# DLRM tower on one core: three field pairs of the first tile are selected by comparison instead of gathered, and the gathers are spaced from round 20 on

## What is computed

```python
e = jnp.stack([tbl_0[ids[:, 0]], ..., tbl_31[ids[:, 31]]], axis=1)   # (2048, 32, 64)
p, q = e[:, ids_x, :], e[:, ids_y, :]                                # all 496 pairs i < j
pw = jnp.einsum('bpi,pij->bpj', p, w)                                # a 64x64 matrix per pair
z = jnp.einsum('bpj,bpj->bp', pw, q)                                 # 496 numbers per row
h = jnp.concatenate([z, dense_ctx], axis=1)                          # 512 numbers
h = jnp.maximum(h @ W_top1 + b_top1, 0.0)                            # 512
h = jnp.maximum(h @ W_top2 + b_top2, 0.0)                            # 256
y = h @ W_top3                                                       # 1
```

## Time and profile before

| | |
|---|---|
| median of 3 runs | 857.16 us |
| the profiled execution's own time | 858.86 us |
| its span, first to last instruction | 857.1 us |
| PE busy | 777.4 us (91%) |
| DVE busy | 614.4 us (72%) |
| POOL busy | 558.9 us (65%), 512 gathers with a mean of 999 ns |
| ACT busy | 276.0 us (32%) |
| granted TensorE clock, mean | 0.98 |

### The profile page before, as it was taken

The page is one execution under the profiler, slowest core; times in us unless marked ns, Lnnn a source line. Parts: engine busy times, 40 slices in busy tenths (PEclk is TensorE's granted clock), DMA queues, the critical chain, the costliest instruction groups (busy, mean ns, idle before and its releaser), DMA issues. The chain is left out here.

```text
span 857.1 us, 10074 instructions
## 1 busy us (share of the span) xinstructions
PE 777.4 (91%) x3904; PEld 284.5 (33%) x3904; DVE 614.4 (72%) x514; ACT 276.0 (32%) x461; POOL 558.9 (65%) x564
## 2 busy tenths in 40 slices
PE   0167999999999968999998999999998999999988
PEld 0022333333333323333333333333333333333333
DVE  0045778777887855988976788888877689889840
ACT  1253323213345211512454322503444422511102
POOL 6777777777777777778877788878877881101000
PEclk9988999999999988999999999999999999999999
DMA  4512222223322236757879577757879477827400
GB/s 131 203 33 71 76 76 65 66 73 76 76 77 74 57 96 141 164 136 161 199 166 219 123 168 167 158 144 158 192 160 231 105 167 151 172 49 141 93 13 0
DMA packets 33846, 103.44 MB, mean 121 GB/s; under 512 B 10564, under 2 KB 10948, under 8 KB 27528
## 3 DMA queue, kind: packets, MB, share of 16 engines
q0 software_dynamic: 23296, 67.14, 38.7%
q1 hardware_dynamic: 10504, 35.67, 13.5%
HBM read 52.43 MB, written 0.01 MB: 61 GB/s over the span
## 5 line engine op out<-in xcount | busy, mean ns | idle before, releaser
L582 DVE TENSOR_TENSOR prod<-main_ps,quad_t 128x1024 f32<-128x1024 f32 x448 | 517.4, 1216 | 193.4 <-PE main_ps L476 193.1
L348 POOL DMA_INDIRECT emb<-in_tbl,idx x512 | 511.6, 999 | 158.7 <-issue 152.8
L475 PE MATMUL main_ps<-e_t,w_sb 64*128 64x512 f32 x992 | 467.8, 610 | 0.0
L476 PE MATMUL main_ps<-e_t,w_sb 64*128 64x512 f32 x992 | 467.8, 610 | 0.0
L475 PEld LDWEIGHTS main_ps<-e_t,w_sb 64*128 64x128 f32 x992 | 176.8, 188 | 245.7 <-issue 175.1
L510 PE MATMUL z_ps<-prod,const_sb 128*32 128x512 f32 x1456 | 190.4, 605 | 22.2 <-DMA prod<-prod 19.0
L476 PEld LDWEIGHTS main_ps<-e_t,w_sb 64*128 64x128 f32 x992 | 176.8, 188 | 0.0
L613 ACT ACTIVATE e_t<-x_ps 128x512 f32<-128x512 f32 x64 | 38.3, 599 | 337.8 <-PE x_ps L446 332.3
L624 ACT ACTIVATE quad_t<-x_ps 32x512 f32<-32x512 f32 x224 | 131.4, 587 | 2.7
L359 POOL DMA_DIRECT2D prod<-prod x48 | 47.1, 981 | 92.1 <-DVE prod L582 92.0
L446 PE MATMUL x_ps<-const_sb,emb 128*128 128x128 f32 x256 | 44.7, 300 | 52.9 <-DMA emb<-in_tbl,idx 52.9
(11 more groups left out here) (18 smaller groups left out, 110.6 us busy)
## 6 DMA issues: line engine op xcount, KB each, us to landing
prod<-prod POOLq DMA_DIRECT2D x48, 1024.0 KB, 8.3
w_sb<-in_w SPq DMA_DIRECT2D x65, 512.0 KB, 4.1
emb<-in_tbl,idx POOLq DMA_INDIRECT x512
w_sb<-in_w SPq DMA_DIRECT2D x1, 1024.0 KB, 12.5
z_sb<-in_ctx SPq DMA_DIRECT2D x32, 4.0 KB
idx<-in_ids SPq DMA_DIRECT2D x1, 192.0 KB, 10.1
const_sb<-in_const SPq DMA_DIRECT2D x1, 125.0 KB, 2.2
idx<-in_ids SPq DMA_DIRECT2D x1, 64.0 KB, 1.9
```

The source lines that it names most:

```text
L348: pool.indirect_dma_start(out=emb[:, PLACE[n] + s // 2, s % 2, odd * EMBED:(odd + 1) * EMBED], out_offset=None, in_=tables[f], in_offset=b ...
L475: nc.tensor.matmul(main_ps[:, slot, c], w_sb[LOW, u, :], e_duo(t, low)[LOW, :], start=True, stop=True)
L476: last = nc.tensor.matmul(main_ps[:, slot + 1, c], w_sb[UP, u, :], e_duo(t, up)[UP, :], start=True, stop=True)
L582: ins = nc.vector.tensor_tensor(prod[:, a:a + 2, :], main_ps[:, slot:slot + 2, :], quad_t[:, quad_slot(t, q), h:h + 1, :].to_broadcast([P, ...
```

## The change

The file is also tidied (the code for half-width tiles goes, `step` becomes `unit`, the ids are laid out in another order); these parts issue the same instructions. What differs:

- Duos 13, 12 and 11 of the first tile are not gathered. SP loads their six tables whole (1000 or 1250 rows, 8 or 10 rows to each of 125 partitions) and their ids, one row spread to all partitions, into buffers that the MLP uses later. For each of the 8 or 10 rows that a partition holds, DVE compares 512 ids with that row's number (`compare_duo`, 125x512, 50 of them), which gives ones and zeros in the last quarter of `prod`. PE multiplies 125x64 of the table by it (`select_duo`) and sums over the rows in PSUM: in two banks of `main_ps` and in `z_ps`, which are not in use yet.
- The order in which the duos of the first tile are brought in becomes 13, 15, 12, 14, 11, 10, ... (`ARRIVE`); POOL gathers 15, 14, 10, 9, ...
- From round 20 of the first tile on POOL issues at most 4 gathers a round (before: from round 32 on).
- Rounds 0, 1, 4 and 6 of the second tile are folded by DMA too: 52 folds.
- The first MLP step waits for the last quarter of z and its context rows only ahead of its fourth matmul.

```diff
+COMPARED = (13, 12, 11)
+CHUNK = 125
+TABLE_ROWS = {26: 1000, 27: 1000, 24: 1250, 25: 1000, 22: 1000, 23: 1000}
+OH_PAIRS = 4
+OH_STEPS = [(m, k, [x for x in range(2) if k < CHUNKS[2 * m + x]]) for m in COMPARED
+            for k in range(max(CHUNKS[2 * m], CHUNKS[2 * m + 1]))]
+ARRIVE = (13, 15, 12, 14, 11, *range(10, -1, -1))
...
-UNFOLDED = {0: range(32), 1: (0, 1, 2, 3, 4, 6, 11, 19, 27), 2: (3, 11, 19, 27), 3: (3, 11, 19, 27, 30, 31)}
+UNFOLDED = {0: range(32), 1: (3, 11, 19, 27), 2: (3, 11, 19, 27), 3: (3, 11, 19, 27, 30, 31)}
...
-POOL_GATHERS = 4
+FREE_ROUNDS, POOL_GATHERS = 20, 4
...
-                    for _ in range(min(room, POOL_GATHERS) if a >= NGROUP else room):
+                    for _ in range(room if NGROUP * t + n < FREE_ROUNDS else min(room, POOL_GATHERS)):
...
+            def load_compared(i):
+                m = COMPARED[i]
+                at = TILE * COMPARED_FIELDS.index(2 * m)
+                sp.dma_start(z_flat[:, at:at + 2 * TILE].bitcast(I32), ids_c[i:i + 1, :].partition_broadcast(P)).then_inc(compare_in[i], 16)
+                for f in (2 * m, 2 * m + 1):
+                    sp.dma_start(table(f), tables[f].rearrange("(p k) e -> p (k e)", p=CHUNK)).then_inc(compare_in[i], 16)
+
+            sp.dma_start(idx[:, 0, :], ids[:, 0, :]).then_inc(idx_in[0], 16)
+            sp.dma_start(const_sb[:, :], const).then_inc(const_in, 16)
+            load_compared(0)
+            load_compared(1)
             load_weights(0)
-
-            sp.wait_ge(gathered[0], GATHERED[0])
+            load_compared(2)
+
+            sp.wait_ge(gathered[0], 16 * DUO_GATHERS)
...
+            def select_duo(m):
+
+                pe.wait_ge(compare_in[COMPARED.index(m)], 3 * 16)
+                bank = duo_bank(0, m)
+                mine = [i for i, step in enumerate(OH_STEPS) if step[0] == m]
+                for i in mine:
+                    _, k, xs = OH_STEPS[i]
+                    pe.wait_ge(hot_made, OH_MADE[i])
+                    for x in xs:
+                        f = 2 * m + x
+                        last = nc.tensor.matmul(bank[EMBED * x:EMBED * x + EMBED, :], table(f)[:, EMBED * k:EMBED * k + EMBED], hot(i, x),
+                                                start=(k == 0), stop=(k == CHUNKS[f] - 1))
+                    last.then_inc(hot_used, 1)
+                pe.wait_ge(hot_used, mine[-1] + 1)
+                pe.nop(nofuse=True).then_inc(transposed, 1)
...
-                        if n == 0 and k == 0:
-                            pe.wait_ge(z_out, Z0[t + 1])
...
+                        if n == 0 and k in (0, KTILES - 1):
+                            pe.wait_ge(z_out, KTILES * (t + 1) - (k == 0))
+
+                            rows = len([g for g in STARS if (g // ROUNDS_KT == KTILES - 1) == (k == KTILES - 1)])
+                            pe.wait_ge(ctx_in[k == KTILES - 1], 16 * 2 * rows * (t + 1))
...
+            def compare_duo(m):
+
+                if m == COMPARED[0]:
+                    dve.wait_ge(const_in, 16)
+                dve.wait_ge(compare_in[COMPARED.index(m)], 3 * 16)
+                for i, (d, k, xs) in enumerate(OH_STEPS):
+                    if d != m:
+                        continue
+                    if i >= OH_PAIRS:
+
+                        dve.wait_ge(hot_used, i - OH_PAIRS + 1)
+                    for x in xs:
+                        f = 2 * m + x
+                        at = P + 122 + IOTA[CHUNKS[f]] + k
+                        nc.vector.tensor_scalar(hot(i, x), compared_ids(f)[0:CHUNK, :], const_sb[0:CHUNK, at:at + 1], None, ALU.is_equal)\
+                          .then_inc(hot_made, 1)
```

More of the change, by code:

```diff
@@ L8 @@
 P = 128
[L9 to L12, removed]
+TILE = 512
+TILES = BATCH // TILE
+SUBS = TILE // P
 DUOS, QUADS = FIELDS // 2, FIELDS // 4
@@ L178, in order_events @@
     for t in range(TILES):
[L179 to L183, removed]
+        at, last = {}, 0
+        for m in ARRIVE if t == 0 else range(DUOS - 1, -1, -1):
+            j = DUOS - 1 - m
+            if t == 0:
+                n = max(min(FIRST_DUO[m] - 1, unit0(DUO_AT[j] + 1) if j > 12 else NUNIT), 0)
+            else:
+                n = min(unit0(NGROUP * t + DUO_AT[j]), NUNIT * t + FIRST_DUO[m])
+            at[m] = last = max(n, last)
             put(at[m], ("duo", t, m))
@@ L408, in _ @@
                 if kind == "end":
[L409 to L413 removed]
+                    part = PARTS_TILE * t + n // 2 + W_PARTS
+                    if n % 2 and part < PARTS_TILE * TILES:
+                        load_weights(part)
@@ L438, in transpose_duo @@
             def transpose_duo(t, m):
[L439 to L452 removed]
+                n = RING[t, m]
@@ L477, in main_products @@
[L477 to L490 removed]
+                elif n == MAIN - 1:
+                    pe.wait_ge(evicted, max(EVICTED["duo", 0, m] for m in COMPARED[:2]))
@@ new lines, in main_products @@
+                slot, w = 2 * (n % MAIN), (NGROUP * SLOTS4 * t + SLOTS4 * g + p) % W_SLOTS
+                kind, what = GROUPS[g]
+                if kind == "low":
+                    low = up = what[p % 2][0]
+                else:
+                    low, up = (side[0] // 2 for side in star_units(*what)[p])
+                nc.tensor.matmul(main_ps[:, slot, :], w_sb[LOW, w, :], e_duo(low)[LOW, :], start=True, stop=True)
+                nc.tensor.matmul(main_ps[:, slot + 1, :], w_sb[UP, w, :], e_duo(up)[UP, :], start=True, stop=True).then_inc(mains, 1)
@@ L547, in _ @@
             pe.wait_ge(const_in, 16)
-            for kind, a, b in EVENTS:
-                if kind == "duo":
-                    transpose_duo(a, b)
-                elif kind == "step":
-                    main_products(a, b)
+            for kind, t, n in EVENTS:
+                if kind == "duo" and (t, n) in RING:
+                    transpose_duo(t, n)
+                elif kind == "duo":
+                    select_duo(n)
+                elif kind == "unit":
+                    main_products(t, n)
@@ new lines, in product @@
+                slot, s = 2 * (n % MAIN), prod_tile(G, p, 0)
+                nc.vector.tensor_tensor(prod[:, s:s + 2, :], main_ps[:, slot:slot + 2, :], e_q, ALU.mult).then_inc(products, 1)
+                if (t, g) in V_FOLDS and p == 3:
+                    dve.wait_ge(products, n + 1)
+                    s = prod_tile(G, 0, 0)
+                    nc.vector.tensor_tensor(prod[:, s:s + 4, :], prod[:, s:s + 4, :], prod[:, s + 4:s + 8, :], ALU.add).then_inc(v_folded, 1)
+            for kind, t, n in EVENTS:
+                if kind == "duo" and (t, n) not in RING:
+                    compare_duo(n)
+                elif kind == "unit":
+                    product(t, n)
```

549 lines of the change are left out of this document (244 added, 305 removed).

## The result

| | before | after |
|---|---|---|
| median of the runs, us | 857.72 (855.94 to 859.48, 4 runs) | 829.61 (828.68 to 830.96, 4 runs) |
| span / own time of the profiled execution, us | 857.1 / 858.86 | 826.7 / 828.68 |
| PE busy | 91% | 95% |
| gathers, DMA folds | 512, 48 | 488, 52 |
| POOL issues its first DMA fold at, us | 316.89 | 241.94 |

After over before is 0.9674, with a 95% interval of 0.9649 to 0.9698: 28.1 us, 3.3% faster. Forecast: 833, range 823 to 849. The two profiled executions lie further apart, 30.2 us: that of after is the fastest of its four, and that of before is 1.7 us over the median that the prediction started from.

A forecast was written before the change was run, and what follows sets the result against it. POOL's queue up to the last fold PE waits for (654.79), then landing and PE alone, was taken as the bound: 857.1 - 35.0 + 4.6 + 9 - 2.4 = 833.3, forecast 833 us, range 823 to 849.

The forecast's parts named there:

- Gathers, 35.0 us: POOL's queue: 28 fewer gathers ahead of the folds, at 1.25 us each, bring the folds 35.0 us earlier.
- Four folds, 4.6 us: POOL's queue: four more folds ahead of the last that matters, 1.16 us each, make it 4.6 us later.
- Comparisons, 9 us: DVE against POOL: gathers beginning during a comparison wait for the rest of it; 9 us lost, possible 0 to 34.
- rival A: DVE against POOL: comparisons don't touch POOL and gathers beside them keep 0.95 us; 824 us, chance 0.20.
- POOL's last fold that matters: POOL's fold issued at 654.79 comes earlier by 35.0 - 4.6 - 9; PE reduces it at 643.4 instead of 664.77.
- The end, 2.4 us: PE before its first MLP matmul: three matmuls fit in the 2.40 us gap; 2.4 us gained, bounded by 0 and 2.4.
- The start: First tile: comparisons begin at about 8 us, duo 9 is transposed at 65 instead of 75.06, PE 10 us earlier.
- PE has 18 us in hand: At the last fold: PE alone would reduce it at 625.2, POOL lets it at 643.4, so POOL decides.
- rival C: POOL and DVE take turns, comparisons waiting for running gathers; PE ends at 866, decides once duo 9 passes 83; chance 0.11.
- This wait costs nothing, since POOL goes on: Round 0's new fold: landed at 255, wanted by PE at 249; the wait was counted as free.
- B: DVE against POOL: comparisons shut POOL out for all their time, 31 to 34 us; 855 to 858, chance 0.14.
- D: PE's selection is the brake: 26 pairs at 1.7 us, 44 us instead of 22; no change of the forecast.

The follow-up runs named there:

- experiment 1: The changed kernel with 24 gathers issued again by POOL at the end of the first tile, into a buffer nobody reads: 857.6 us, ratio 1.0004.
- experiment 3: The changed kernel with gathers unlimited up to round 32 again, as before the change: 833.9 us, ratio 0.9733.
- Experiment 2: The changed kernel with rounds 0, 1, 4 and 6 of the second tile not folded, as before the change: 826.0 us, ratio 0.9634.
- experiment 7: The changed kernel with the comparison as a TENSOR_TENSOR of two SBUF operands in place of TENSOR_SCALAR: 826.8 us, ratio 0.9651.
- Experiment 12: The changed kernel with each tile's first MLP matmul waiting again for all sums and all context rows: 833.9 us, ratio 0.9723.
- Experiment 4: The changed kernel with tables and ids of the compared duos loaded only after duo 15's gathers have landed: 834.0 us, ratio 0.9727.
- experiment 9: experiment 5 with duo 11's comparisons and selection also put ahead of the first product: 812.9 us, ratio 0.9477.
- experiment 8: The changed kernel with 48 unused comparisons more, three a round behind products in rounds 4 to 19 of the first tile: 833.1 us, ratio 0.9707.
- experiment 5: The changed kernel with at most 3 gathers a round in rounds 20 to 39: 822.0 us, ratio 0.9588.
- experiment 11: experiment 9 with the comparison written with two operands in SBUF: 819.0 us, ratio 0.9551.
- experiment 6: The kernel before the change, without comparisons, with gathers unlimited to round 20, 3 a round in rounds 20 to 39, then 4: 840.8 us, ratio 0.9806.

## Why the prediction was right, and where it wasn't

The forecast held, and by its cause: POOL's queue decides (experiment 1), and the time follows its last fold that matters. Several terms had the wrong size, one place was misread, and in one place two errors happened to cancel.

- *Gathers, 35.0 us.* Experiment 1 shows 30 of them (29.9 at the first fold, 28.0 in the time) and experiment 3 the other 5 (4.3 in both).
- *Four folds, 4.6 us.* Experiment 2 gives 3.6 in the time and 5.0 at the fold of round 8. Right in sign, and nearly in size.
- *Comparisons, 9 us: mis-sized.* 3.1 us measured. Two halves of the estimate were wrong. A comparison takes 0.40 in a row and 0.49 alone, not 0.62 and 0.65: I scaled from DVE's two-tensor instructions, which experiment 7 shows to be the slower form (0.62 and 0.70). And a gather that begins within them doesn't wait for one to end, it is only 0.24 to 0.34 us longer; ten such gathers are nearly all of the 3.1. The prediction had set the forecast apart from rival A at 4 us lost, so by this cost A (up to 3 us) was as near as the forecast, though its gathers of 0.95 are refuted. With 3.1 in place of 9 the sum gives 827.5, 2.1 us under the measured median. The estimate of 0.43 us that the prediction worked out from the Trainium skill (VectorE: DVE Perf Modes, the perf-mode tier table) was nearer than mine. The Trainium skill (SBUF — State Buffer, Who interferes with whom) says that the one that comes second is blocked for all of the other's instruction: ten comparisons in a row took 4.05 us across three gathers, so DVE was not held up, and POOL lost about 0.3 us on a gather that met them. There the measurement decides. The same section of the Trainium skill has two-tensor instructions contend only with what GpSimd reads, and expects descriptor writing to be free of them; that fits 34 comparisons of experiment 7 with one longer gather, but neither the one that is longer nor the gathers lengthened beside DVE's folds, which are two-tensor instructions too.
- *POOL's last fold that matters.* The sum had it 21.4 us earlier (35.0 - 4.6 - 9), the trace 25.5, 4.1 more. 5.9 of that are the comparisons' (9 - 3.1). 0.9 more come from gathers beside DVE's own folds ahead of round 8's fold: those at 275.29 and 300.93 were 3.1 us too long before, one at 265.59 is 2.2 us too long after. Behind it, the same kind of gather costs 2.7: between round 8's fold and the last that matters POOL issues 228 gathers and 33 folds in both kernels, in 337.9 us before and 340.65 after. The sum took that stretch as unchanged, but which gather meets a fold of DVE's shifts with time. 5.9 + 0.9 - 2.7 = 4.1.
- *The end, 2.4 us: too small.* 4.1. I bounded it by the gap and didn't see that the 15.67 us behind it had the low clock in it: without a gap the same 32 matmuls take 14.08. Experiment 12 shows both parts. I had used this effect for the wait of 11.46 us, and left it out here. (With the 4.1 above, 1.7 here and 0.8 for the last fold's landing, the span is 6.6 us under the sum's 833.3; the median is only 3.8 under the forecast, since the profiled execution of before was above its median and that of after the lowest of four.)
- *The start.* Comparisons begin at 13.79, not 8: two tables and ids are there later than 1 MB at 4.1 us a half led to expect. They end sooner by their own speed, DVE then stands idle 8.88 us for duo 14's copy, and duo 9 is transposed at 64.50 (65 forecast). Two errors that cancel, and that was luck.
- *"PE has 18 us in hand": wrong.* Experiment 4 used 11.8 of them and lost 4.4 us, so there were 7.4. I had compared PE and POOL at the last fold, as if POOL's queue only ran ahead. But a fold at the head of the queue waits for PE's products, and a wait there isn't made up: all gathers behind it are later. The slack is what there is at the first fold, and it was some 7 us. Duo 9 could have come 7 us later, near 72, and not at 83 as rival C had it. The forecast was spared this only because the start came out as planned.
- *The new folds' waits.* "This wait costs nothing, since POOL goes on" held for the wait at 250.52; that round 8's fold would be the place where PE waits did not (301.81 has none). PE's waits moved to 250.52, 258.10 and the runs of consecutive folds, and round 8 profited from them.

Rival A (824) had the comparisons at nothing; they cost 3.1. B and C are refuted by the gathers' 1.2 to 1.3 us and by comparisons whose only gaps within a duo (0.36 to 0.92 us) are waits for PE. D is refuted too: in experiment 9 PE selects duo 11, 8 pairs of matmuls (x32, four instructions a pair), in 7.09 us, 0.89 a pair and not 1.7. In the changed kernel duo 13's 8 pairs take 8.53, beside the comparisons that they wait for.

Open: why single gathers beside comparisons are much longer than the others (2.47 us in experiment 8, 1.68 in experiment 5), why experiment 8 lost only 3.4 us for a first fold 5.5 us later, and 2 of the 6 us of experiment 11.

## What to carry to other kernels

A queue that also waits has slack only where it first meets what it waits for; work out the margin there, not at its end. When an engine's queue decides, moving entries behind the binding one helps as removing them does, and it is free (4.3 us for 4 gathers in experiment 3, and 7.6 and 16.6 us for one line in experiments 5 and 6), until another engine decides. A gap on PE can cost more than its length, in slower matmuls behind it.

## What the runs showed of the hardware

- A comparison of one int32 tensor in SBUF with a scalar, 512 columns, took 0.49 us alone and 0.40 in a row. Of 17 gathers beside such comparisons on POOL ten took 1.19 to 1.29 us instead of 0.95; single ones took 1.68 (experiment 5) and 2.47 (experiment 8). With two tensors a comparison took 0.70 and 0.62, and at most one gather of a burst was longer (1.40 and 1.33 in experiment 7, none in experiment 11). The form that is faster on DVE is the dearer one for POOL.
- One comparison of 0.48 us lengthened the gather that met it as much (1.22) as a whole row of them did.
- Two tensors in a longer instruction do lengthen a gather: beside DVE's folds of 2048 columns, before and after, single gathers took 1.4 to 3.2 us (the one at 290.00 took 2.91).
- A gap of 2.5 us ahead of 32 matmuls made them 15.67 us instead of 14.08. But the gap's length alone doesn't tell whether the clock falls. In the changed kernel the reduction at 258.10 has a gap of 2.88 us ahead of it, takes 1.06, and the granted clock stays at 1.00. In experiment 5 one with 2.91 takes 1.94:

```profile
630.83 1.94 PE L518 MATMUL z_ps<-prod,const_sb 128*32 128x512 f32 x8 [2.91 <-DMA prod<-prod]
```

  The clock can also fall a little later: in experiment 3 the reduction at 636.97, behind a gap of 1.80 us, takes 1.07, and from 638 to 642 us the granted clock is 0.60 and 0.54. In the changed kernel none of the gaps ahead of reductions (up to 2.88 us) did this.
